# Narrow diagonal tiles behind the products with V, side tasks sorted by the engine that empties their bank, lower parts of queries and keys made behind the next maximum

## The chip, the cores and the metric

The program runs on one core of one Trainium2 chip. The metric is the device time of one execution in microseconds (us). Engines are named as the profile names them: PE is TensorE, DVE is VectorE, ACT is ScalarE, POOL is GpSimd, SP is SyncE, which here only issues transfers.

## The reference

A block of four layers on an input of 2 sequences x 2048 tokens x 256 channels, each with a layer norm ahead of it and a residual sum behind it. The change touches the third, causal attention with 16 heads of 64 channels:

```python
latent_kv = x @ w_kv_down                      # 256 -> 128
k, v = split(latent_kv @ w_kv_up)              # 128 -> 2 x 1024
q = x @ w_q                                    # 256 -> 1024
att = einsum('bqhd,bkhd->bhqk', q, k) * 64 ** -0.5
att = softmax(where(causal, att, -inf))
y = einsum('bhqk,bkhd->bqhd', att, v) @ w_out  # 1024 -> 256
```

Ahead of it stand a state-space layer and a gated token-mixing layer, behind it the token-mixing layer again.

## The kernel before

**Units, tiles and steps.** Attention works on two heads (a pair) and a block of 512 queries at a time: a unit. A sequence has 8 pairs and 4 blocks, so there are 64 units. The unit of block j takes 4(j+1) steps, one for each tile of 128 keys, so a pair has 4 + 8 + 12 + 16 = 40 steps and the whole attention 640. The order of a unit's tiles is the list `TILE[j]`. The last four tiles (numbers 4j to 4j+3) lie on the diagonal: the first of them is as wide as any other (512 queries), the others have 384, 256 and 128. All four need VectorE to lay the causal limit over 128 columns of the scores (`limit`, L1150) before the exponential.

**One step.** The score (L926 to L932): four products for each of the two heads, of the upper and lower parts of keys and queries (`k_hi`, `k_lo`, `q_hi`, `q_lo`) and of the negative maximum, into two PSUM banks. ScalarE takes the exponential into one of four `prob` buffers (L1359), TensorE multiplies it with V into the bank `heads_out` (L947, "weigh"), GpSimd sums it for the denominator (L1438, L1440, L1443, "accumulate").

**Maxima.** Before a unit's scores, its row maxima are taken, some 20 steps ahead: for each tile of 128 queries and block of keys one rough score from the upper parts alone (L903), into banks 5 and 6 (`two_heads`), which VectorE reduces (L1141, and on the diagonal L1138 twice). There are 640 maxima too. They all use this one pair of banks, so a maximum on TensorE waits until VectorE has reduced the maximum before.

**Rounds.** `Plan.attention` writes every engine's order by hand, in rounds of four steps (s = 0, 4, ...). TensorE's order in round s, as a rule:

1. maximum, score s+2, score s+3, maximum (called first and second maximum below)
2. weigh s, s+1, s+2, s+3
3. maximum, score s+4, score s+5, maximum (third and fourth)
4. up to four side tasks ("fillers")

Scores s+4 and s+7 use banks 0 and 1, scores s+5 and s+6 banks 2 and 3. If no side task is open, the fourth maximum is left out and the next round has three maxima. Places are named below by s modulo 40, so a pair has ten rounds, 0, 4, ..., 36; a pair's own steps begin in round 36, whose third part holds its steps 0 and 1.

**Side tasks.** Queries, keys, values, turned maxima, the projection of a unit's result in two halves (`project`), and, once a sequence, latents and turned tiles. In a pair there are 4 queries, 4 keys, 4 turned maxima, 8 halves of projections and on average 4 halves of values. Each has a round from which it is open and one in which it is due. The bank of each is given by its place in the round, `SIDE = [7, 0, 1, 7]`: the first one open goes into bank 7, a second if it is due within 16 steps into bank 0, a third within 8 steps into bank 1, a fourth within 4 into bank 7. A side task in bank 0 or 1 waits for the exponential of step s+4, and score s+7 waits until the side task's bank is emptied. Values and turned maxima are emptied by ScalarE, projections by VectorE (a sum into `X`, L1183). Queries and keys are emptied by both: ScalarE copies the upper part (L1327, L1333), and then VectorE makes the lower part from the bank and the upper part (L1124, L1129).

**Other work on VectorE in the rounds.** `load_out` makes the lower part of the next output weights (L1110), once a pair, ahead of the first maximum; "chores" (`pair_lo`, `values_lo`) make those of other weights behind a maximum; `invert` takes a reciprocal (L1164).

**Ends of a unit.** ScalarE takes the result out of `heads_out` (L1365); 8 steps later GpSimd scales it; 12 steps later `two_parts` splits it, upper part on ScalarE (L1376), lower part on GpSimd (L1452), queued behind the accumulate of step s+1. Projections are open from the next round on.

Of the kernel before, what the change touches and what calls it, by code (L numbers as in the profile page):

```python
# [30 lines left out]
LEAD = 20  # L31
NDEN, QUAD = 8, 32
NG = 3
SIDE = [7, 0, 1, 7]
TILE = [[0, 1, 2, 3], [0, 1, 4, 5, 2, 3, 6, 7], [0, 1, 2, 8, 3, 4, 5, 9, 6, 7, 10, 11], [0, 1, 2, 12, 3, 4, 5, 13, 6, 7, 8, 14, 9, 10, 11, 15]]
DVE_OUT = 62
MIX = [(1, 0), (1, 1), (0, 0), (0, 1)]

# [10 lines left out]
UNITS = [(b, p, j) for b in range(NB) for p in range(NPAIR) for j in range(NBLK)]  # L49
# [30 lines left out]
class Plan:  # L80
# [7 lines left out]
    def __init__(self):  # L88
        self.tasks, self.bank = [], {}
        self.normal, self.stats, self.roots, self.acc = {}, {}, {}, {}  # L90
        self.n_normal = self.n_stats = self.n_roots = self.n_acc = self.step = self.turn = 0
        self.count = [0] * 8
        self.in_steps, self.layers_done, self.done, self.chores = False, False, set(), []
        self.side_bank, self.max_bank = 7, 5
        self.kinds, self.nth, self.masked = {}, {}, {}
        self.start, self.step_of, self.at = [], {}, 0
        self.maxima = [(idx, c, t) for idx, (_, _, j) in enumerate(UNITS) for c in range(j + 1) for t in range(TPB)]
        for idx in range(NU):
            self.start.append(len(self.step_of))
            for t in range(TPB * (UNITS[idx][2] + 1)):  # L100
                self.step_of[idx, t] = len(self.step_of)
        self.freed = [None] * 8
        self.phases()
# [24 lines left out]

    def add(self, *task):
        kind = task[0]  # L130
        self.tasks.append(task)
        self.normal[task] = self.n_normal
        self.kinds[kind] = self.kinds.get(kind, 0) + 1
        self.nth[task] = self.kinds[kind]
        if kind in ("ssm_normal", "turn_normal"):
            self.n_normal += TPB
        elif kind in ("ssm_front", "turn"):
            self.take(task, *([(7,)] * CH if self.in_steps else self.any_bank(CH)))
        elif kind in ("tail_norm", "att_normal"):
            self.n_normal += 2  # L140
        elif kind in ("ssm_states", "ssm_output", "update"):
            self.take(task, *self.any_bank(2))
        elif kind == "products":
            self.take(task, *self.any_bank(4))
        elif kind in ("x_stats", "g_stats"):
            self.stats[task] = self.n_stats
            self.n_stats += 1
        elif kind == "inverse_std":
            self.n_roots += 1
            self.roots[task] = self.n_roots  # L150
        elif kind in ("query", "key", "value", "turn_max", "latent", "denominators", "turn_tiles", "project"):
            self.take(task, self.one_bank())
        elif kind == "maximum":
            self.take(task, (self.max_bank, self.max_bank + 1))
        elif kind == "score":
            n = (0, 2, 2, 0)[self.step_of[task[1:]] % 4]
            if tile_of(*task[1:]) >= TPB * UNITS[task[1]][2]:
                self.masked[task[1:]] = len(self.masked) + 1
            self.take(task, (n, n + 1))
        elif kind == "accumulate":  # L160
            _, idx, t = task
            x0 = left_of(idx, t)
            if t:
                self.n_acc += 2 if t == 1 and x0 else 1
            self.acc[idx, t] = self.n_acc
# [140 lines left out]
    def need(self, *task):  # L306
# [4 lines left out]
        kind = task[0]  # L311
        if kind == "turn_tiles":
            _, b, t = task
# [10 lines left out]
        elif kind == "value":  # L324
            _, vn, half = task
            n, j = divmod(vn, NBLK)
# [15 lines left out]
        elif kind == "maximum":  # L342
            _, idx, c, t = task
            self.need("query", idx)
            self.need("key", idx - UNITS[idx][2] + c)
        elif kind == "fetch_pair" and task[1] >= 2:
            assert all((k, (task[1] - 1) * NBLK - 1) in self.done for k in ("query", "key"))
        elif kind == "fetch_out" and task[1] >= 2:
# [26 lines left out]
            self.chores += [("pair_lo", task[1], i) for i in range(2)]  # L375
        if kind == "load_values":
            self.chores.append(("values_lo", task[1]))

    def chore(self, task):
        self.chores.remove(task)  # L380
# [37 lines left out]
    def attention(self):  # L418
# [22 lines left out]
            if self.chores:  # L441
                self.chore(self.chores[0])

        def filler(latest):
            open_ = sorted((x for x in fillers if x[0] <= s and x[2] not in self.done and early(x[2])), key=lambda x: x[1])
            if open_ and open_[0][1] <= latest:
                fillers.remove(open_[0])
                self.need(*open_[0][2])

        def output(idx):  # L450

# [13 lines left out]
        def early(task):  # L465

            return self.layers_done or task[0] in ("turn_tiles", "latent") or task[1] < {"key": 2, "query": 2, "turn_max": 2, "value": 1}.get(task[0], 0)

        def rows(first, goal, spaced):

            if self.at < goal:
                maximum()
            for n, step in enumerate(steps[first:first + 2]):
                if n and self.at < goal - 1:
                    maximum()
                self.need("score", *step)
            if self.at < goal and spaced:
                maximum()
            else:
                chore()  # L480

        for s in range(-4, len(steps), 4):
# [6 lines left out]
            if s >= 0:  # L489
                goal = min(len(self.maxima), s + 4 + LEAD) if self.layers_done else 0  # L490
                rows(s + 2, goal, True)
                if not s:
                    self.heads_free = self.freed[4]
                for idx, t in steps[s:s + 4]:
                    self.need("weigh", idx, t)
                    self.need("accumulate", idx, t)
                    if (idx, t) == steps[s + 1]:
                        due("two_parts")
                    if t == TPB * (UNITS[idx][2] + 1) - 1:
                        self.need("take_out", idx)  # L500
                        output(idx)
                due("denominators")
                due("scale_out")
                if not s:
                    self.in_steps = False
                    yield
                    self.in_steps = True
            urgent = max([self.start[i] + TPB * (UNITS[i][2] + 1) for i in range(NU) if self.start[i] <= s + 8])
            goal = min(len(self.maxima), max(urgent, s + 6 + LEAD)) if self.layers_done else self.at
            rows(s + 4, goal, any(x[0] <= s and x[2] not in self.done for x in fillers))  # L510
            for n, self.side_bank in enumerate(SIDE):
                filler((10 ** 6, s + 16, s + 8, s + 4)[n])
            self.side_bank = 7
            if self.layers_done and self.at < min(len(self.maxima), s + LEAD):
                maximum()
# [23 lines left out]
def build(nc, u, wA, wF, wKD, wQuery, wValue, wOut, aDiag, h0, gb, mu, out):  # L539
# [4 lines left out]
    with ExitStack() as ctx:  # L544
# [427 lines left out]
        def vector_program(ve):  # L972
# [18 lines left out]
            for task in tasks:  # L991
# [124 lines left out]
                elif kind == "latent":  # L1116
# [1 line left out]
                    cols = slice(j * BLK, (j + 1) * BLK)  # L1118
                    w.wait_ge(lat_hi_ok, b * NBLK + j + 1)
                    ve.tensor_tensor(lat_lo[:, cols], bank(task), lat_hi[:, cols], ALU.subtract).then_inc(empty(task)[0], 1)  # L1120
                elif kind == "query":
                    idx = task[1]
                    w.wait_ge(q_hi_ok, plan.nth[task])
                    ve.scalar_tensor_tensor(out=q_lo[idx % NQ][:, :], in0=bank(task), scalar=DH ** -0.5, in1=q_hi[idx % NQ][:, :],  # L1124
                                            op0=ALU.mult, op1=ALU.subtract).then_inc(empty(task)[0], 1)
                elif kind == "key":
                    idx = task[1]
                    w.wait_ge(k_hi_ok, plan.nth[task])
                    ve.tensor_tensor(k_lo[idx % NKS][:, :], bank(task), k_hi[idx % NKS][:, :], ALU.subtract).then_inc(empty(task)[0], 1)  # L1129
# [431 lines left out]
```

## Time and profile before

| | us |
|---|---|
| median of 3 runs | 2225.58 |
| lowest, highest | 2222.75, 2227.15 |
| profiled execution, its own time | 2222.64 |
| its span in the profile | 2221.3 |
| mean granted TensorE clock (1 is full) | 0.971 |

The span is from the first to the last instruction of the profiled execution; 1.3 us of its time lie around it. Times below count from the start of the span. The attention's rounds run from about 290 us to about 2100 us; a pair takes 109 to 123 us. "Idle before" is the time for which an engine did nothing before an instruction, and the arrow names what ended it.

### The profile page before, as it was taken

To read this page: it belongs to the slowest core of one execution; us is meant where nothing else is said; L and a number is where in the kernel's file an instruction comes from. 1 tells how busy PE (TensorE), PEld (TensorE's weight loads), DVE (VectorE), ACT (ScalarE), POOL (GpSimd) and SP (SyncE) were. 2 spreads that over 40 slices of the span, in tenths; PEclk is the share of its full clock that TensorE was granted. 3 is DMA by queue.
4 is the path that set the end of the run, shared out by engine and by line. 5 is a ranking of instruction groups with operands and counts; after the bars stand their busy time and mean duration, and the time that the engine had idled before them with its cause. 6 is when DMAs were issued, how large, how long until landed. Compare 5 with 4: busy or idle time off the path is not lost.

```text
span 2221.3 us, 33667 instructions
## 1 busy us (share of the span) xinstructions
PE 2004.8 (90%) x12886; PEld 1257.5 (57%) x12886; DVE 1323.7 (60%) x2728; ACT 1077.5 (49%) x1596; POOL 1423.1 (64%) x812
## 2 busy tenths in 40 slices
PE   8987688888999999999988998999899989998889
PEld 6765455545555655555555655555456555554566
DVE  7876655656666555555655556565656565655353
ACT  5775444434444444444454544444444444544575
POOL 1433235776777777777756686766677777777822
PEclk9999799999999999999998999999999999999999
DMA  3000000000000000000000000000000000000001
GB/s 118 1 1 1 0 7 13 17 13 9 18 12 18 9 18 12 18 10 18 12 18 9 11 19 11 17 11 19 11 17 11 19 10 17 11 13 11 25 24 57
DMA packets 29232, 36.90 MB, mean 17 GB/s; under 512 B 6928, under 2 KB 20368, under 8 KB 29072
## 3 DMA queue, kind: packets, MB, share of 16 engines
q1 hardware_dynamic: 29072, 34.76, 5.1%
q8 instruction: 102, 1.67, 0.3%
q14 instruction: 58, 0.48, 0.1%
HBM read 30.02 MB, written 4.46 MB: 16 GB/s over the span
## 4 chain that ended last, share of the span: by engine, by line
PE 54%; DVE 19%; ACT 11%; POOL 9%; issue 6%; DMA 1%; SPq 0%; ACTq 0%; POOLq 0%; DVEq 0%
PE heads_out L947 19%; PE scores L752 7%; PE two_heads L903 7%; POOL acc L1443 6%; PE beside L752 5%; ACT prob L1359 5%; DVE part_max L1141 4%; PE scores L926 3%; PE scores L932 3%; PE scores L930 3%; PE scores L928 3%; DVE two_heads L1138 2%; DVE stats L986 2%; PE two_heads L752 1%; PE beside L958 1%
## 5 line engine op out<-in xcount | busy, mean ns | idle before, releaser
L1443 POOL TENSOR_TENSOR acc<-acc,prob 128x1024 f32<-128x1024 f32 (+3 forms) x512 | 1015.5, 1983 | 236.0 <-ACT prob L1359 189.7
L1359 ACT ACTIVATE prob<-scores 128x1024 f32<-128x1024 f32 (+3 forms) x640 | 550.6, 896 | 632.9 <-PE scores L932 308.8
L1141 DVE TENSOR_REDUCE part_max<-two_heads 128x2 f32<-128x1024 f32 x384 | 468.4, 1220 | 324.7 <-PE two_heads L903 324.1
L947 PE MATMUL heads_out<-prob,V 128*64 128x512 f32 (+3 forms) x2560 | 531.9, 559 | 7.2 <-ACT prob L1359 7.0
L903 PE MATMUL two_heads<-k_hi,q_hi 64*128 64x512 f32 (+3 forms) x1280 | 284.6, 440 | 122.8 <-DVE part_max L1141 78.2
L1138 DVE CUSTOM_DVE_ANT_0 two_heads<-two_heads,mask 128x128 f32<-128x128 f32 (+3 forms) x512 | 241.1, 512 | 250.7 <-PE two_heads L903 250.6
L947 PEld LDWEIGHTS heads_out<-prob,V 128*64 128x64 f32 x2560 | 176.1, 142 | 319.0 <-issue 300.3
L926 PE MATMUL scores<-q_hi,k_hi 64*128 64x512 f32 (+3 forms) x1280 | 246.0, 379 | 30.5 <-ACT prob L1359 17.4
L903 PEld LDWEIGHTS two_heads<-k_hi,q_hi 64*128 64x128 f32 x1280 | 121.2, 185 | 262.6 <-DVE part_max L1141 110.8
L930 PE MATMUL scores<-q_lo,k_hi 64*128 64x512 f32 (+3 forms) x1280 | 236.6, 363 | 0.0
L932 PE MATMUL scores<-neg_max,sel 64*128 64x512 f32 (+3 forms) x1280 | 236.6, 363 | 0.0
L928 PE MATMUL scores<-q_hi,k_lo 64*128 64x512 f32 (+3 forms) x1280 | 236.4, 363 | 0.0
L1438 POOL TENSOR_TENSOR acc<-prob 128x768 f32<-128x768 f32 (+1 forms) x64 | 144.4, 2257 | 126.7 <-ACT prob L1359 103.1
L1452 POOL TENSOR_TENSOR oT_lo<-oT,oT_hi 128x512 fp32r<-128x512 f32 x62 | 78.7, 1269 | 141.8 <-ACT oT_hi L1376 141.8
L926 PEld LDWEIGHTS scores<-q_hi,k_hi 64*128 64x128 f32 x1280 | 123.0, 186 | 77.5 <-issue 26.6
L932 PEld LDWEIGHTS scores<-neg_max,sel 64*128 64x128 f32 x1280 | 123.2, 186 | 18.9
L930 PEld LDWEIGHTS scores<-q_lo,k_hi 64*128 64x128 f32 x1280 | 123.1, 186 | 18.7
L928 PEld LDWEIGHTS scores<-q_hi,k_lo 64*128 64x128 f32 x1280 | 123.1, 186 | 17.0
L1150 DVE TENSOR_TENSOR scores<-scores,limit 128x256 f32<-128x256 f32 x256 | 105.1, 430 | 26.8 <-PE scores L932 26.2
L1365 ACT ACTIVATE oT<-heads_out 128x512 f32<-128x512 f32 x64 | 38.3, 598 | 125.9 <-PE heads_out L947 114.4
L1370 ACT ACTIVATE den_rows<-beside 128x256 f32<-128x256 f32 x64 | 24.6, 384 | 133.7 <-PE beside L958 133.7
L1448 POOL TENSOR_TENSOR oT<-oT,rden 128x512 f32<-128x512 f32 x62 | 79.9, 1289 | 1.9 <-DMA rden<-rden_rows 1.6
(295 smaller groups left out, 2884.1 us busy)
## 6 DMA issues: line engine op xcount, KB each, us to landing
rden<-rden_rows SPq DMA_DIRECT2D x128, 128.0 KB, 2.9
X<-u SPq DMA_DIRECT2D x8, 512.0 KB, 8.9
out<-X SPq DMA_DIRECT2D x8, 512.0 KB, 2.9
wQK_raw<-wQuery SPq DMA_DIRECT2D x16, 192.0 KB, 3.1
wO_raw<-wOut SPq DMA_DIRECT2D x16, 128.0 KB, 2.8
wV_raw<-wValue SPq DMA_DIRECT2D x8, 128.0 KB, 2.7
den<-den_rows SPq DMA_DIRECT2D x64, 4.0 KB
rden_rows<-den SPq DMA_DIRECT2D x64, 4.0 KB, 1.3
```

Of the source, the lines that this page charges most:

```text
L752: made = pe.matmul(dst, l, r, start=first and n == 0, stop=last and n == len(pairs) - 1)
L903: made = pe.matmul(pair_of(task)[:, h, 0:width], q[head(h), t * P:(t + 1) * P], k[head(h), 0:width], start=True, stop=True)
L926: pe.matmul(scores[:, first + h, x0:], k_hi[g][head(h), kc], q_hi[i][head(h), x0:], start=True, stop=False)
L928: pe.matmul(scores[:, first + h, x0:], k_lo[g][head(h), kc], q_hi[i][head(h), x0:], start=False, stop=False)
L930: pe.matmul(scores[:, first + h, x0:], k_hi[g][head(h), kc], q_lo[i][head(h), x0:], start=False, stop=False)
L932: made = pe.matmul(scores[:, first + h, x0:], sel[head(h), :], neg_max[idx % NMAX][head(h), x0:], start=False, stop=True)
L947: made = pe.matmul(heads_out[head(h), x0:], V[vn % NVS][:, tt, p % 2, head(h)], prob[step % NPROB][:, h, x0:], start=t == 0, stop=t == TPB ...
L1138: made = ve.tensor_tensor_reduce(out=pair_of(task)[:, h, 0:width], in0=pair_of(task)[:, h, 0:width], in1=mask[:, BLK - width:], scale=1.0, ...
L1141: made = ve.reduce_max(part_max[:, t, :, c:c + 1], pair_of(task)[:, :, 0:width], AX.X)
L1359: ac.activation(prob[step % NPROB][:, :, x0:], scores[:, first:first + 2, x0:], ACT.Exp).then_inc(empty(task)[0], 1)
L1438: po.tensor_tensor(total[:, :, x0:], old[:, :, x0:], new[:, :, x0:], ALU.add).then_inc(acc_ok, 1)
L1443: po.tensor_tensor(total[:, :, x0:], total[:, :, x0:], new[:, :, x0:], ALU.add).then_inc(acc_ok, 1)
```

## The change

- `TILE`: the narrow diagonal tiles (384, 256 and 128 wide) move to odd places 1, 5, 9, 13 of their unit where they can, so that they are mostly a round's step s+5 in place of its step s+3. Blocks 0 and 1 keep some at even places.
- `SIDE`: each of four places takes only certain kinds. Place one: a projection, into bank 0. Place two: query, key, latent or turned tiles, into bank 7. Place three: value, turned maximum or projection, into bank 1. These take whatever is open, however late it is due. Place four: any kind that is due within 4 steps, into the first of banks 0, 1, 7 that this round has not used.
- A query or key that went into bank 7 no longer has its lower part made by VectorE at its own place in the order; a task `lower` does it behind the first maximum of the next round, or sooner if a task that uses bank 7 or the score's operands asks for it.
- `two_parts` is queued behind the accumulate of step s+2 in place of s+1.

```diff
-SIDE = [7, 0, 1, 7]
-TILE = [[0, 1, 2, 3], [0, 1, 4, 5, 2, 3, 6, 7], [0, 1, 2, 8, 3, 4, 5, 9, 6, 7, 10, 11], [0, 1, 2, 12, 3, 4, 5, 13, 6, 7, 8, 14, 9, 10, 11, 15]]
+SIDE = [([0], ("project",), 99), ([7], ("query", "key", "latent", "turn_tiles"), 99), ([1], ("value", "turn_max", "project"), 99), ([0, 1, 7], None, 4)]
+TILE = [[0, 3, 1, 2], [0, 1, 4, 5, 2, 7, 3, 6], [0, 1, 2, 8, 3, 11, 4, 9, 5, 10, 6, 7], [0, 1, 2, 12, 3, 15, 4, 5, 6, 14, 7, 8, 9, 13, 10, 11]]
...
     def add(self, *task):
         kind = task[0]
+        if self.lowers and self.side_bank == 7 and kind in ("turn_tiles", "latent", "turn_max", "denominators", "query", "key", "value", "project"):
+            self.lower()
...
+            if self.lowers & {("query", idx), ("key", idx - UNITS[idx][2] + c)}:
+                self.lower()
...
+    def lower(self):
+
+        pending, self.lowers = sorted(self.lowers), set()
+        for task in pending:
+            self.add("lower", *task)
+
...
             if self.at < goal:
                 maximum()
+            self.lower()
             for n, step in enumerate(steps[first:first + 2]):
...
-                    if (idx, t) == steps[s + 1]:
+                    if (idx, t) == steps[s + 2]:
                         due("two_parts")
...
-            for n, self.side_bank in enumerate(SIDE):
-                filler((10 ** 6, s + 16, s + 8, s + 4)[n])
+            taken = set()
+            for banks, kinds, ahead_by in SIDE:
+                self.side_bank = next((x for x in banks if x not in taken), 7)
+                if filler(s + ahead_by, kinds):
+                    taken.add(self.side_bank)
+                    if self.side_bank == 7 and self.tasks[-1][0] in ("query", "key") and self.layers_done and s + 4 < len(steps):
+                        self.lowers.add(self.tasks[-1])
+                        self.apart.add(self.tasks[-1])
...
-                elif kind == "query":
+                elif kind == "query" and task not in plan.apart or kind == "lower" and task[1] == "query":
+                    task = task[-2:]
...
-                elif kind == "key":
+                elif kind == "key" and task not in plan.apart or kind == "lower" and task[1] == "key":
+                    task = task[-2:]
```

## Rows read from the trace of the kernel before

**Rows 1.** Busy us from 400 to 2040: PE, PEld, DVE, ACT, POOL; clock.

```profile
400.00:2040.00 1640.00, 1507.16 (x10405) 915.41 (x10405) 976.64 (x1977) 744.88 (x1051) 1193.90 (x652) 0.98 0.05 14
```

**Rows 2.** TensorE's waits from 400 to 2040 us: total, times, longest.

```profile
PE two_heads L903 <- DVE part_max L1141: 68.9, 60, 4.1
PE two_heads L903 <- DVE part_max L1138: 29.0, 57, 1.5
PE scores L926 <- ACT prob L1359: 14.4, 15, 1.0
PE scores L926 <- DVE k_lo L1129: 4.1, 7, 0.7
```

**Rows 3.** Timeline of TensorE and VectorE, an ordinary round: start, length.

```profile
1250.04 0.51 PE L903 MATMUL two_heads<-k_hi,q_hi 64*128 64x512 f32 x2 [0.47 <-DVE part_max L1141]
...
1247.76 0.69 DVE L1129 TENSOR_TENSOR k_lo<-scores,k_hi 128x512 fp32r<-128x512 f32 x1 [0.83 <-ACT k_hi L1333]
1248.37 0.53 DVE L1164 RECIPROCAL den<-den 16x64 f32<-16x64 f32 x1
1248.83 1.15 DVE L1141 TENSOR_REDUCE part_max<-two_heads 128x2 f32<-128x1024 f32 x1
```

**Rows 4.** Timeline of VectorE and TensorE, an output weight's lower part.

```profile
1214.10 1.13 DVE L1110 TENSOR_TENSOR wO_lo<-wO_raw,wO_hi 128x256 fp32r<-128x256 f32 x1
...
1216.42 0.50 PE L903 MATMUL two_heads<-k_hi,q_hi 64*128 64x512 f32 x2 [1.35 <-DVE part_max L1141]
1216.85 4.92 PE L947 MATMUL heads_out<-prob,V 128*64 128x512 f32 x16
```

**Rows 5.** Busy time and granted clock in two stretches of weighs.

```profile
1216.80:1221.80 5.00, 5.00 (x20) 1.56 (x18) 1.23 (x1) 1.11 (x2) 3.60 (x3) 0.66 0.00 0
1203.90:1207.40 3.50, 3.50 (x20) 1.12 (x18) 0.89 (x5) 0.77 (x2) 2.56 (x2) 1.00 0.39 112
```

**Rows 6.** Timeline of TensorE, a round with no side task.

```profile
1333.66 0.39 PE L903 MATMUL two_heads<-k_hi,q_hi 64*128 64x512 f32 x2
1335.03 0.50 PE L926 MATMUL scores<-q_hi,k_hi 64*128 64x512 f32 x2 [0.97 <-ACT prob L1359]
...
1337.78 0.49 PE L903 MATMUL two_heads<-k_hi,q_hi 64*128 64x512 f32 x2 [0.93 <-DVE part_max L1141]
```

**Rows 7.** Timeline of TensorE and ScalarE, scores and first side task.

```profile
1244.68 0.39 PE L903 MATMUL two_heads<-k_hi,q_hi 64*128 64x512 f32 x2
1245.00 0.39 PE L752 MATMUL beside<-wO_hi,oT_hi 128*128 128x256 f32 x1
...
1244.01 1.94 ACT L1359 ACTIVATE prob<-scores 128x1024 f32<-128x1024 f32 x2 [1.00 <-PE scores L932]
```

**Rows 8.** Timeline of TensorE, VectorE and ScalarE where a pair begins.

```profile
1232.38 0.40 PE L932 MATMUL scores<-neg_max,sel 64*128 64x512 f32 x2
...
1233.52 0.50 PE L752 MATMUL beside<-att_xT_hi,wQK_hi 128*128 128x512 f32 x1
...
1232.82 0.43 DVE L1150 TENSOR_TENSOR scores<-scores,limit 128x256 f32<-128x256 f32 x1 [0.37 <-PE scores L932]
...
1233.33 1.73 ACT L1359 ACTIVATE prob<-scores 128x1024 f32<-128x1024 f32 x2 [1.15 <-DVE scores L1150]
```

**Rows 9.** Timeline of TensorE, scores 256 and 128 wide.

```profile
1237.79 0.28 PE L926 MATMUL scores<-q_hi,k_hi 64*128 64x256 f32 x2
...
1238.26 0.23 PE L926 MATMUL scores<-q_hi,k_hi 64*128 64x128 f32 x2
...
1238.55 0.28 PE L932 MATMUL scores<-neg_max,sel 64*128 64x128 f32 x2
```

**Rows 10.** Groups, shapes apart: busy, mean ns, idle before.

```profile
L1359 ACT ACTIVATE prob<-scores 128x1024 f32<-128x1024 f32 x448 | 444.8, 1024 | 461.6 <-PE scores L932 308.8 <-DVE scores L1150 77.4 <-POOL acc L1443 75.1
...
L1452 POOL TENSOR_TENSOR oT_lo<-oT,oT_hi 128x512 fp32r<-128x512 f32 x62 | 78.7, 1269 | 141.8 <-ACT oT_hi L1376 141.8
```

**Rows 11.** VectorE's lower part of an output weight: ns min/median/max.

```profile
L1110 DVE TENSOR_TENSOR wO_lo<-wO_raw,wO_hi x16: 349/1490/1772, 330.4 to 1996.3; 128x256 fp32r<-128x256 f32 x16
```

More of the change, by code:

```diff
@@ L95, in __init__ @@
         self.kinds, self.nth, self.masked = {}, {}, {}
+        self.lowers, self.apart = set(), set()
         self.start, self.step_of, self.at = [], {}, 0
@@ L442, in chore, with filler @@
                 self.chore(self.chores[0])
-        def filler(latest):
-            open_ = sorted((x for x in fillers if x[0] <= s and x[2] not in self.done and early(x[2])), key=lambda x: x[1])
+        def filler(latest, kinds=None):
+            open_ = sorted((x for x in fillers if x[0] <= s and x[2] not in self.done and early(x[2]) and (not kinds or x[2][0] in kinds)), key=lambda x: x[1])
             if open_ and open_[0][1] <= latest:
@@ L448, in filler @@
                 self.need(*open_[0][2])
+                return True
         def output(idx):
```

## The prediction

> **What bounds the kernel.** I read the busy times first, for the stretch of the attention alone. TensorE is busy for 1507 of 1640 us, GpSimd for 1194, VectorE for 977 [rows 1]. So TensorE sets the pace, and what can be won is its idle 133 us and what it loses at a lower clock. Then its waits by what ended them: 97.9 us in 117 waits are maxima waiting for VectorE's reduction of the maximum before, 14.4 us are scores waiting for an exponential, 4.1 us for a key's lower part [rows 2].
>
> Then the timeline, to see which maximum waits. It is the second one of a round, between two scores and the products with V. In [rows 3] VectorE waits 0.83 us for ScalarE's upper part of a key, makes the lower part (0.69), takes a reciprocal (0.53) and only then reduces the first maximum; TensorE stands for 0.47 us. The scores between the two maxima are what hides the reduction, and here the second one is narrow. A score 512 wide takes 0.93 us on TensorE (four products of 0.23), 384 wide 0.71, 256 wide 0.47 (1237.79 to 1238.26), 128 wide 0.40 (1238.26 to 1238.66) [rows 9].
>
> I sort the 97.9 us by kind. The lower part of an output weight once a pair: 1.35 us in [rows 4], where it took 1.13; with its median of 1.49 [rows 11] 1.7, and where ScalarE is late more, so about 28 us over the 14.6 pairs of the stretch. Ordinary waits of 0.3 to 0.5 in six rounds of ten and one of 0.93 every other pair [rows 3, 6]: 3.1 us a pair, 45 us. The other 25 us are long waits behind chores, statistics and latents.
>
> **Tile order and deferred lower parts, for the second maximum.** In the changed order the round's scores s+2 and s+3 are both 512 wide in six rounds of ten, and 768 to 896 in sum in most others, where before eight in ten had a narrow one. In [rows 3], without the key's wait and its 0.69, the reduction starts about when the reciprocal is done, some 1248.1, and ends at 1249.3; TensorE comes at 1249.57. Where the pair of scores was 256 and 128 wide it becomes 512 and 256 or more, 0.53 us or more of added cover. Either is more than the usual 0.3 to 0.5. I take all 45 us as gone; the bounds are 30 and 45. The lower part itself (0.69) goes behind the first reduction, where VectorE otherwise stands until the second maximum; nothing asks for it sooner, as queries and keys are made some 28 steps ahead. Uncovered it would cost 0.69 a time.
>
> The output weight's wait stays: `load_out` still stands ahead of the first maximum. Its scores go from 512 and 256 to 512 and 512, so 0.46 us less: 7 us. The other long waits I leave.
>
> A round without side tasks pays 0.97 at a score and 0.93 at the third maximum behind it [rows 6], every other pair. The new sorting gives this round (32) a turned maximum, which was pulled ahead before; the 0.97 goes: 7 us. Keys no longer sit in banks 0 and 1 as a rule: 4 us. Together 63 us, and with the attention's ends 65.
>
> **Side tasks sorted by bank: what it adds.** Before, the first side task took bank 7 and waited for nothing. Now a projection comes first and takes bank 0, which the exponential of step s+4 must leave. [Rows 7] give its distance with a full score s+5: the exponential starts at 1244.01 and takes 1.02 [rows 10], so it ends at 1245.03, and the side task starts at 1245.00. That is 0.05 late at most. But score s+5 is now mostly narrow, and TensorE arrives earlier by just what the score is shorter. Projections fall into rounds 12, 20, 28 and 36:
> - round 12, 128 wide: 0.93 - 0.40 + 0.05 = 0.6
> - round 20, full: 0.05
> - round 28, 256 wide: 0.93 - 0.47 + 0.05 = 0.5
> - round 36, where a pair begins and the exponential waits for the causal limit: it ends at 1233.33 + 1.02 = 1234.35 [rows 8]. The first side task stood at 1233.52 behind a score 384 wide; behind 128 it stands at 1233.21, so it waits 1.2.
>
> The lone turned maximum of round 32, in bank 1 behind a score 384 wide, waits 0.3. That is 2.65 us a pair, 41 us over 15.5 pairs. Behind it the next round's first maximum comes too soon: two maxima can't start closer than about 1.7 us (0.93 + 0.40 + 0.39 in [rows 6]), and 0.3 of maximum, 0.3 of wait and 0.45 of transposes leave 0.6 to wait: 9.5 us. Cost together 50 us; bounds 20, if the exponentials come earlier, and 60.
>
> TensorE's clock page of the Trainium skill ("TensorE: Matmul & The Clock Gate", on why the gap is 56 ns) has a product of 128 columns start 55.6 ns after the one before at full clock, and four of them would make 0.22 us. The trace disagrees: 0.40 [rows 9], and I go by it. By the page the waits in rounds 12 and 36 would grow by 0.18 each, an estimate of 6 us more and a time of 2214.
>
> **The fourth maximum** also has a narrower score ahead. Where that is 128 wide, the third maximum is mostly one 128 or 256 wide on the diagonal, whose reduction is short. I take 0; the bound is 0.2 us in three rounds of a pair, 9 us.
>
> **`two_parts` behind another accumulate.** GpSimd stood 141.8 us before this task, waiting for ScalarE's upper part [rows 10]; now an addition fills some of that. TensorE waits for GpSimd only through exponentials, little, so I take 0. ScalarE's next take-out may come 0.3 us later: bound 5 us. Shape changes in unit 0's sums move well under 1 us a pair on an engine with slack. No transfer and no wait of the queue on SP is moved past another.
>
> **Clock.** A long wait can be followed by a stretch at the lower level: 16 products took 4.92 us behind the 1.35 us wait [rows 4], at a mean granted clock of 0.66, against 3.5 at 1.00 [rows 5]. A mean of 0.98 [rows 1] means that 4% of the stretch ran at 1.2 GHz and not 2.4, about 32 us lost. Most such waits are long ones, which stay. I take 0; bounds -25, if they vanish, and +22, if the 15 new waits of 1.2 us each bring one at 1.45 us.
>
> **Sum.** 2222.6 - 65 + 50 = 2207.6, against the profiled execution's own time. The median lies 2.9 above that, the profiled one at the low end of the runs, so I say 2209.
>
> **Rivals.**
> - *The side tasks don't wait* (0.20): exponentials come early enough, or the waits replaced others. Then the 65 us stay, 2158, or up to 2180 with half of the waits. For it: the exponential misses a full round by only 0.03 [rows 7]. Against: the arithmetic of widths leaves no room in rounds 12, 28 and 36.
> - *Slower* (0.20): the wait in round 36 is long enough to bring down the clock behind it. The place is the first projection of each pair; the price is 1.45 on top of 1.2. With the fourth maximum's 0.6 the cost per pair becomes 4.7 us, 73 us in all, against 65 won: 2231. It turns at 4.2 us a pair. For it: 1.35 did so in [rows 4]; against: 0.97 and 0.93 in [rows 6] did not.
> - *No change* (0.08): GpSimd, 73% busy, sets the pace of a pair's last unit, and TensorE's won time returns as waits for exponentials: 2223.
> - *The output weight's lower part gets short* (0.05): it takes 0.35 us at the least and 1.49 in the middle [rows 11]. If the shifted sums leave GpSimd idle there, 1.1 a pair goes, 18 us more: 2191. The Trainium skill, "SBUF — State Buffer", on who interferes with whom, names the cause: an operation of VectorE with both inputs in SBUF shares a port with GpSimd's reads, and the loser waits for the other's whole instruction.
> - My forecast (0.47): 2190 to 2220.
>
> **Chances.** Faster by over 0.2% (4.5 us, about what a measurement can tell): 0.47 and 0.05 less 0.05 that lies too near, and 0.20, so 0.67. Same: 0.05 and 0.07 of the 0.08, so 0.12. Slower: 0.20 and the last 0.01, so 0.21. The range takes most of the first rival and the slower one: 2168 to 2236.
>
> **What would show it.** Right: waits of the second maximum near 40 us in place of 98, all long; new waits of side tasks for exponentials, near 40 us, the longest 1.2; q_lo and k_lo without idle time ahead. Wrong: waits for exponentials under 15 us (first rival), or a mean clock under 0.97 (second).

## The result and the profile after

The changed kernel takes 2166.51 us (median of 4 runs, 2162.81 to 2169.17) against 2226.36 for the one before (4 runs): ratio 0.9731, 95% interval 0.9708 to 0.9754. That is 60 us less, just below the range of 2168 to 2236, where 17 us less had been forecast. The profiled execution takes 2169.17 us, 53.5 less than the profiled one before; the mean granted clock rose from 0.971 to 0.978.

First the page, part 1, of the changed kernel, and the view of busy time by stretch (PE, PEld, DVE, ACT, POOL, granted clock). The stretch ends at 1990 us, since TensorE has then had as many instructions as before the change at 2040 (10398 and 10405):

```profile
PE 1978.3 (91%) x12886; PEld 1251.4 (58%) x12886; DVE 1328.0 (61%) x2728; ACT 1074.9 (50%) x1596; POOL 1428.5 (66%) x812
```

```profile
400.00:1990.00 1590.00, 1479.84 (x10398) 908.51 (x10396) 980.77 (x1984) 743.76 (x1051) 1196.56 (x651) 0.99 0.05 14
```

For the same work as in [rows 1] TensorE is idle for 110.2 us and not 132.8, and busy for 1480 and not 1507. Two things became shorter, and the forecast had only the first. On the whole span the busy time fell from 2004.8 to 1978.3, so 26.5 of the 53.5 us are in it. The same instructions ran; they were faster. Part of that is the clock: (1 - clock) times the span, the time lost at 1.2 GHz as an estimate, falls from 64 us (0.971 of 2221.3) to 48 us (0.978 of 2167.9). The other 10 us are taken up below, behind no_side.

TensorE's waits in that stretch (total, times, longest):

```profile
PE two_heads L922 <- DVE part_max L1162: 37.0, 37, 2.7
PE scores L771 <- ACT prob L1380: 33.9, 57, 1.1
PE two_heads L922 <- DVE part_max L1159: 8.7, 24, 1.3
PE beside L771 <- DVE q_lo L1144: 5.2, 7, 1.0
PE scores L945 <- ACT prob L1380: 3.5, 6, 0.6
PE two_heads L922 <- DVE q_lo L1144: 3.0, 2, 1.5
PE beside L868 <- DVE k_lo L1150: 2.8, 2, 1.4
```

Against [rows 2]: maxima wait 45.7 us and not 97.9, scores 3.5 and not 18.5. New are 33.9 us of side tasks waiting for exponentials, and 11 us in which something waits for the lower part of a query or key. The timeline of TensorE shows the new waits in one pair (start, length, in brackets the idle time and what ended it):

```profile
1299.43 0.38 PE L771 MATMUL scores<-wO_hi,oT_hi 128*128 128x256 f32 x1 [0.29 <-ACT prob L1380]
1304.18 0.49 PE L922 MATMUL two_heads<-k_hi,q_hi 64*128 64x512 f32 x2 [0.77 <-DVE part_max L1162]
1310.38 0.66 PE L930 MATMUL scores<-ident,row_max 128*128 128x128 f32 x4 [0.27 <-ACT prob L1380]
1311.54 0.49 PE L922 MATMUL two_heads<-k_hi,q_hi 64*128 64x512 f32 x2 [0.50 <-DVE part_max L1162]
1320.37 0.38 PE L771 MATMUL scores<-wO_hi,oT_hi 128*128 128x256 f32 x1 [1.07 <-ACT prob L1380]
```

They are rounds 28 (a projection), 32 (the second maximum, then the lone turned maximum and the maximum behind it) and 36 (a projection). Round 12 of an earlier pair:

```profile
1127.69 0.39 PE L771 MATMUL scores<-wO_hi,oT_hi 128*128 128x256 f32 x1 [0.64 <-ACT prob L1380]
```

The forecast had 0.5 for round 28, 0.3 and 0.6 for the turned maximum of round 32 and the maximum behind it, 1.2 for round 36 and 0.6 for round 12; the trace has 0.29, 0.27, 0.50, 1.07 and 0.64. The second maximum of round 32, the one behind the output weight's lower part, is where the forecast was far off: 0.77 and not some 1.5.

### The profile page after: what moved, and what is told of

It is laid out like the page before. It is cut to its first block, busy times and chain, and to the rows that moved or that the text cites. A ratio compares the mean times of both kernels' runs of the same rounds, so it can differ in the third digit from the quotient of the medians.

```text
span 2167.9 us, 33697 instructions
## 1 busy us (share of the span) xinstructions
PE 1978.3 (91%) x12886; PEld 1251.4 (58%) x12886; DVE 1328.0 (61%) x2728; ACT 1074.9 (50%) x1596; POOL 1428.5 (66%) x812
## 4 chain that ended last, share of the span: by engine, by line
PE 70%; DVE 16%; ACT 9%; issue 3%; POOL 1%; DMA 1%; SPq 0%; ACTq 0%; DVEq 0%; POOLq 0%
PE heads_out L966 22%; PE scores L771 11%; PE two_heads L922 8%; PE beside L771 6%; PE scores L945 4%; PE scores L951 4%; PE scores L949 4%; PE scores L947 4%; ACT prob L1380 4%; DVE part_max L1162 3%; DVE two_heads L1159 2%; PE two_heads L771 2%; PE beside L977 2%; DVE stats L1005 2%; DVE X L1204 1%
## 5 line engine op out<-in xcount | busy, mean ns | idle before, releaser
L1464 POOL TENSOR_TENSOR acc<-acc,prob 128x1024 f32<-128x1024 f32 (+3 forms) x512 | 1034.8, 2021 | 368.7 <-ACT prob L1380 330.9
L966 PE MATMUL heads_out<-prob,V 128*64 128x512 f32 (+3 forms) x2560 | 517.3, 546 | 3.8 <-ACT prob L1380 3.7
L966 PEld LDWEIGHTS heads_out<-prob,V 128*64 128x64 f32 x2560 | 167.9, 139 | 278.4 <-issue 241.4
L945 PE MATMUL scores<-q_hi,k_hi 64*128 64x512 f32 (+3 forms) x1280 | 239.9, 370 | 9.1 <-ACT prob L1380 6.7
L1459 POOL TENSOR_TENSOR acc<-prob 128x256 f32<-128x256 f32 (+1 forms) x64 | 126.7, 1980 | 78.5 <-ACT prob L1380 77.7
L1171 DVE TENSOR_TENSOR scores<-scores,limit 128x256 f32<-128x256 f32 x256 | 106.2, 428 | 63.0 <-PE scores L951 61.2
L1204 DVE TENSOR_TENSOR X<-X,scores 128x512 f32<-128x512 f32 x127 | 87.0, 686 | 82.0 <-PE scores L771 80.8
L771 PE MATMUL scores<-wO_hi,oT_hi 128*128 128x256 f32 x254 | 79.0, 311 | 31.9 <-ACT prob L1380 31.4
```

The source lines that it names most:

```text
L771: made = pe.matmul(dst, l, r, start=first and n == 0, stop=last and n == len(pairs) - 1)
L945: pe.matmul(scores[:, first + h, x0:], k_hi[g][head(h), kc], q_hi[i][head(h), x0:], start=True, stop=False)
L966: made = pe.matmul(heads_out[head(h), x0:], V[vn % NVS][:, tt, p % 2, head(h)], prob[step % NPROB][:, h, x0:], start=t == 0, stop=t == TPB ...
L1459: po.tensor_tensor(total[:, :, x0:], old[:, :, x0:], new[:, :, x0:], ALU.add).then_inc(acc_ok, 1)
L1464: po.tensor_tensor(total[:, :, x0:], total[:, :, x0:], new[:, :, x0:], ALU.add).then_inc(acc_ok, 1)
```

## The experiments

All were timed in 3 rounds beside the kernel before on the same chip. "Maxima" is the sum of TensorE's waits for VectorE's reductions over the whole span in the run's view of waits, "exp." that of the group of L752 (projections and other products; L766 to L773 in the variants) waiting for an exponential, "out lo" the median length of VectorE's operation for the output weight's lower part (`wO_lo`).

| run | us | ratio, 95% interval | clock | maxima us | exp. us | out lo ns |
|---|---|---|---|---|---|---|
| before | 2226.36 | 1 | 0.971 | 122.0 | 0.3 | 1490 |
| after | 2166.51 | 0.9731, 0.9708 to 0.9754 | 0.978 | 68.1 | 36.6 | 1216 |
| tile_only | 2167.61 | 0.9765, 0.973 to 0.98 | 0.982 | 90.2 | 0.6 | 1566 |
| side_only | 2251.6 | 1.0139, 1.0104 to 1.0175 | 0.967 | 123.0 | 15.4 | 2378 |
| lower_only | 2238.33 | 1.0074, 1.0051 to 1.0097 | 0.965 | 121.5 | 0.3 | 2212 |
| two_only | 2223.54 | 1.0009, 0.9988 to 1.0029 | 0.966 | 115.7 | 0.3 | 426 |
| no_tile | 2203.99 | 0.9899, 0.9881 to 0.9918 | 0.967 | 96.6 | 15.6 | 1631 |
| no_side | 2163.32 | 0.9717, 0.9699 to 0.9736 | 0.977 | 73.4 | 0.6 | 590 |
| no_lower | 2191.58 | 0.9846, 0.9831 to 0.9861 | 0.979 | 75.9 | 36.0 | 719 |
| no_two | 2161.94 | 0.9744, 0.9709 to 0.978 | 0.978 | 59.2 | 36.1 | 526 |
| after_stall | 2198.92 | 0.988, 0.9861 to 0.9899 | 0.972 | 89.4 | 36.6 | 1444 |
| before_out_chore | 2191.37 | 0.9863, 0.9831 to 0.9895 | 0.971 | 95.7 | 0.3 | 862 |
| before_out_pool | 2187.08 | 0.9856, 0.9826 to 0.9886 | 0.973 | 95.1 | 0.3 | on GpSimd |
| after_out_chore | 2148.7 | 0.9668, 0.9637 to 0.9699 | 0.984 | 55.1 | 36.1 | 946 |
| after_swap | 2136.68 | 0.9617, 0.9578 to 0.9657 | 0.977 | 68.6 | 11.0 | 1218 |
| after_swap_out | 2121.96 | 0.9548, 0.9509 to 0.9586 | 0.979 | 57.4 | 10.5 | 950 |
| after_swap_pool | 2110.77 | 0.9512, 0.9483 to 0.9542 | 0.982 | 50.1 | 12.6 | on GpSimd |
| no_side_pool | 2145.82 | 0.967, 0.9643 to 0.9698 | 0.98 | 61.2 | 2.7 | on GpSimd |

The runs were timed in sets, and the kernel before had medians of 2220.84 to 2226.36 in them, so runs of different sets are compared by their ratios. The clock and the last three columns are those of the profiled execution.

### One part of the change alone

**tile_only**: the `TILE` line of the change, everything else as before.

> The kernel before with the new tile order alone. First theory (waits of the second maximum are covered by the wider scores ahead of it, and nothing is paid at side tasks because the first of them still takes bank 7): the second maximum's 98 us of waits fall to about 50, no side task waits for an exponential, and with about half of the low-clock stretches gone the time is 2170 to 2182. Rival (the tile order only moves the wait to the fourth maximum, and the gain comes from the deferred lower parts): 2212 to 2226.

2167.61 us: the tile order alone gives what the whole change gives. Maxima wait 32 us less, side tasks wait 0.6 us in all for an exponential, and the clock is 0.982. The first theory holds in its main point; the time lies 2 us below its range. Its sizes were off: between 400 and 1990 us the maxima still wait 67.9 us (52.0 and 15.9) and not about 50, and the clock gives more. The stretches at 1.2 GHz between 400 us and the end of that work are 16 before, 6 here and 6 after the change.

**side_only**: the `SIDE` line and its loop, without `self.lowers.add` and `self.apart.add`.

> The kernel before with the new sorting of side tasks alone: old tile order, lower parts at once. First theory (a projection in bank 0 waits for the exponential of step s+4 only where score s+5 is narrow or the exponential is late by the causal limit): waits of side tasks of about 15 us, nearly all in the round where a pair begins, against 10 to 15 us won at rounds without side tasks: 2212 to 2226. Rival (sorting by the emptying engine is what frees VectorE): 2180 to 2200.

2251.6 us, slower than either theory. The side tasks' 15 us are as expected. What was missing stands in the last column: the output weight's lower part takes 2.38 us and not 1.49. The second maximum behind it waits about 2.4 us and not about 2, though other maxima win that back (123.0 us in all against 122.0). The rest of the loss is busy time, 2018.2 us against 2004.8, in part at the lower clock (0.967).

**lower_only**: the deferral in the old loop.

```diff
             for n, self.side_bank in enumerate(SIDE):
-                filler((10 ** 6, s + 16, s + 8, s + 4)[n])
+                if filler((10 ** 6, s + 16, s + 8, s + 4)[n]):
+                    if self.side_bank == 7 and self.tasks[-1][0] in ("query", "key") and self.layers_done and s + 4 < len(steps):
+                        self.lowers.add(self.tasks[-1])
+                        self.apart.add(self.tasks[-1])
```

> The kernel before with deferred lower parts alone, for queries and keys that the old sorting puts into bank 7. First theory (only some queries and keys are in bank 7 there, and the narrow scores ahead of the second maximum remain): waits of the second maximum fall by 10 to 20 us, time 2200 to 2215. Rival (VectorE's wait for ScalarE's upper part is the cause of most waits): they fall by 40 us or more, 2165 to 2185.

2238.33 us, 0.7% slower; both theories fall. The maxima wait as long as before, and again the output weight's operation grew, to 2.21 us. The timeline of VectorE and of GpSimd in this run shows what its length hangs on:

```profile
1090.86 2.52 DVE L1126 TENSOR_TENSOR wO_lo<-wO_raw,wO_hi 128x256 fp32r<-128x256 f32 x1 [0.58 <-ACT wO_hi L1316]
...
1090.72 2.38 POOL L1461 TENSOR_TENSOR acc<-acc,prob 128x1024 f32<-128x1024 f32 x1
```

VectorE's operation begins 0.14 us after an addition of GpSimd and ends 0.28 us after it (1093.38 and 1093.10). In the kernel before, same place of the program:

```profile
1082.72 1.72 DVE L1110 TENSOR_TENSOR wO_lo<-wO_raw,wO_hi 128x256 fp32r<-128x256 f32 x1 [0.59 <-ACT wO_hi L1298]
...
1081.77 2.38 POOL L1443 TENSOR_TENSOR acc<-acc,prob 128x1024 f32<-128x1024 f32 x1
```

It begins later in the addition and ends again 0.29 us after it (1084.44, 1084.15). In the changed kernel:

```profile
1059.15 1.19 DVE L1129 TENSOR_TENSOR wO_lo<-wO_raw,wO_hi 128x256 fp32r<-128x256 f32 x1
...
1057.67 2.39 POOL L1464 TENSOR_TENSOR acc<-acc,prob 128x1024 f32<-128x1024 f32 x1
```

Later still, and the same 0.28 us behind. This operation has both inputs in SBUF. Alone it takes 0.35 us at the least [rows 11]; beside an addition it lasts until 0.28 us behind the addition's end, so its length is what is left of that addition. Each edit that shifts one engine against the other changes it, and with it the wait of the second maximum. So the one-part runs below and above never change one thing alone: the last column of the table has to be read with each.

**two_only**: `steps[s + 1]` becomes `steps[s + 2]` for `two_parts`.

> The kernel before with two_parts behind the accumulate of step s+2 alone. First theory: GpSimd's idle time before this task falls from 142 us to under 20, and TensorE doesn't notice: 2220 to 2229. Rival (GpSimd's delay reaches VectorE through ScalarE's late upper parts, and so the maxima): 2195 to 2212.

2223.54 us, no difference that can be measured, and GpSimd's idle time before this task falls to 7.4 us, as the first theory has it. But TensorE does notice; the effects cancel. The output weight's operation:

```profile
L1124 DVE TENSOR_TENSOR wO_lo<-wO_raw,wO_hi x16: 350/426/2503, 330.1 to 1999.4; 128x256 fp32r<-128x256 f32 x16
```

The median of 0.43 us hides two kinds of pair: from the fourth on it takes 0.42 to 0.43 us in seven and 2.45 to 2.50 us in five. The second maximum behind it waits 0.8 us in six of the seven and 2.8 us in the five. TensorE's idle time is 8 us less than before, its busy time 7 us more, at a clock of 0.966.

### The change without one part

**no_tile, no_side, no_lower, no_two**: the changed kernel with the old `TILE` line; with the old sorting, the deferral kept as in lower_only; without the two lines that add to `self.lowers` and `self.apart`; with `steps[s + 1]`.

> The changed kernel with the old tile order. First theory (the tile order brings most of the gain and most of the side tasks' waits): waits of side tasks for exponentials fall from 35 us to about 15, waits of the second maximum rise to 65 to 80, time 2190 to 2210. Rival (the other parts carry the gain): 2162 to 2175.

2203.99 us: the other three parts give 1.0% together, the tile order the rest. The first theory holds: exponentials 15.6 us, maxima 74.3 us (59.2 and 15.1) between 400 and 2025 us.

> The changed kernel with the old sorting of side tasks. First theory (the new sorting costs some 35 us of waits for exponentials and wins some 15 to 20): side tasks wait under 3 us, time 2145 to 2165. Rival (the sorting is needed for the gain, since it puts all queries and keys into bank 7): 2172 to 2195.

2163.32 us, the same as the change within the intervals, though the side tasks' 36 us are gone. So the sorting wins about as much as it costs. I had it winning 11 us. TensorE's busy time has the difference: in this run it is idle 22.5 us less than after the change and busy 17.4 us more (1995.7 against 1978.3), at nearly the same clock. Part of the 22.5 is the output weight's operation, 0.59 us here against 1.22. In tile_only, also with the old sorting, busy times by stretch are:

```profile
400.00:1990.00 1590.00, 1492.45 (x10367) 901.68 (x10365) 982.50 (x1971) 746.39 (x1048) 1197.11 (x649) 0.99 0.05 14
```

12.6 us more than after the change, for 31 instructions fewer, at the same clock. One source can be seen. With the old sorting a score is held up by a query's lower part in its bank so shortly that no idle time is recorded. TensorE before the change, with the round 8 in which `q_lo` in bank 0 ends at 1269.54:

```profile
1269.14 0.39 PE L932 MATMUL scores<-neg_max,sel 64*128 64x512 f32 x2
1269.60 0.50 PE L926 MATMUL scores<-q_hi,k_hi 64*128 64x512 f32 x2
1269.93 0.39 PE L928 MATMUL scores<-q_hi,k_lo 64*128 64x512 f32 x2
```

Start to start is 0.46 us where a product takes 0.23: 0.23 us lost, hidden behind the modelled end of the product before.

Busy time less the clock's part, estimated for each profiled execution as in the section on the result, sorts the runs: 1940 us before, 1953 in tile_only, 1946 in no_side, 1945 in no_lower, but 1931 after the change and 1929 in no_tile. New sorting and deferral together take some 10 us of such hold-ups out of the kernel before and some 20 out of tile_only. That all of it is this one kind of hold-up is not shown.

> The changed kernel with lower parts made at once. First theory (the wider scores already cover the reduction in most rounds, so deferring adds little): 2168 to 2180. Rival (deferring is what removes the waits): 2190 to 2210.

2191.58 us, in the rival's range: in company with the new sorting and the new tile order the deferral is worth 1.2%. The profiled executions are 18.6 us apart; 12.4 us of that are busy time and 6.2 idle, so most of it is hidden hold-ups and not, as the rival has it, waits. The maxima wait only 8 us longer here, but that is with an output weight's operation of 0.72 us and not 1.22; at the places behind it they wait 7 us less, elsewhere 15 us more. With the old sorting and old tile order the deferral brought no gain (lower_only, where that operation grew).

> The changed kernel with two_parts back behind the accumulate of step s+1. First theory (moving it shifts the phase of GpSimd's additions, and by that the length of VectorE's output-weight operation): that operation's length changes from 1.24 us to another value between 0.4 and 2.5 us and the second maximum's wait in round 32 changes by the same amount; time 2150 to 2190, in proportion to it. Rival (GpSimd's order is without effect on VectorE): 1.24 us stays and the time is 2163 to 2170.

2161.94 us, and `wO_lo` takes 0.53 us and not 1.22, the maxima's waits fall by 9 us. The phase of GpSimd's additions shifted and shortened VectorE's operation, as the first theory has it. A gain in time can't be told: by ratio the run is no faster than the change (0.9744 against 0.9731, intervals overlapping).

### The wait behind the output weight

**before_out_chore** and **after_out_chore**: VectorE makes this lower part behind a maximum.

```diff
         if kind == "load_values":
             self.chores.append(("values_lo", task[1]))
+        if kind == "load_out":
+            self.chores.append(("out_lo", task[1]))
...
-                elif kind == "load_out":
+                elif kind == "out_lo":
```

(the second edit in the program of VectorE alone)

> The kernel before with one edit: VectorE makes the output weight's lower part behind a maximum, as it does with the other weights, and no longer ahead of the first maximum of the round. First theory (this one wait, once a pair, costs its 2 us and the low clock behind it): idle time falls by 20 to 28 us and the time in low-clock stretches by another 12 to 20, time 2180 to 2195. Rival (idle time alone): 2198 to 2206.

2191.37 us: one wait a pair, 26 us of idle time in all, was worth 31. The idle time and the time are as in the first theory. Its clock part isn't there in its size: the profiled executions have the same clock (0.971), and busy times of 2002.1 and 2004.8 us.

> The changed kernel with the same edit. Its wait there is 0.8 us and no low-clock stretch follows it. First theory: only the idle time goes, 12 us, 2152 to 2158. Rival (it brings clock too): under 2148.

2148.7 us, 0.6% less than the change; the waits fall by 13 us. It lies between the theories: the idle time of the first, and a little clock besides (0.984 in the profiled execution, the fastest of four; 0.980 to 0.982 in the others).

**before_out_pool**: the same operation on GpSimd, at its old place in the order.

```diff
-                    ve.tensor_tensor(wO_lo[n % 2][:, :], wO_raw[n % 2][:, :], wO_hi[n % 2][:, :], ALU.subtract).then_inc(wO_ok, 1)
+                    po.tensor_tensor(wO_lo[n % 2][:, :], wO_raw[n % 2][:, :], wO_hi[n % 2][:, :], ALU.subtract).then_inc(wO_ok, 1)
```

> The kernel before with one edit: GpSimd in place of VectorE makes the output weight's lower part, at the same place of the task order. First theory (this operation on VectorE lasts until the addition that GpSimd is in has ended, and that is what the second maximum waits for): on GpSimd it takes under 0.8 us each time, the second maximum's wait in round 32 falls from 2.1 us to 0.3 or less, idle time falls by 25 to 30 us and the time is 2182 to 2194. Rival (the wait comes from ScalarE's late upper part and from the projections' sums): the wait in round 32 stays above 0.8 us and the time above 2205.

2187.08 us. This operation's view (ns min/median/max):

```profile
L1443 POOL TENSOR_TENSOR wO_lo<-wO_raw,wO_hi x16: 722/738/743, 328.2 to 1965.4; 128x256 fp32r<-128x256 f32 x16
```

On GpSimd it always takes 0.72 to 0.74 us, and TensorE's idle time falls by 26 us, as the first theory has it. But the run doesn't part the two theories: with the operation VectorE also loses its standing for ScalarE's upper part, the 0.59 us in the row at 1082.72. That was 8.2 us in 12 times before the change. The other part, VectorE held by GpSimd, is what its operation takes beyond 0.42 us, some 14 us over the 16 pairs.

**after_stall**: the reverse, idle time put back.

```diff
                 elif kind == "load_out":
                     n = task[1]
                     w.wait_ge(wO_hi_ok, n + 1)
+                    w.wait_ge(att_const, 4)
+                    for i in range(2):
+                        ve.reduce_max(spare[:, i:i + 1], mask[:, :], AX.X)
```

> The changed kernel with two reductions of a constant into an unused column added on VectorE once a pair, just ahead of the output weight's lower part, about 1.25 us. They lengthen the wait of the second maximum there from 0.8 us to about 2.0, what it was before the change; nothing else is changed. First theory (the waits above about 1.3 us are what brings TensorE to the lower clock): 15 x 1.25 = 19 us more idle time and 10 to 22 us more in low-clock stretches, which go from 7 to 15 or more between 400 and 2040 us; 2197 to 2207. Rival (the clock came back because all idle time together shrank): idle time alone, 2183 to 2190, and the clock stays at 0.98.

2198.92 us: the maxima wait 21.3 us more, the time is 32 us longer, and the clock falls from 0.978 to 0.972. The time and its division are the first theory's: a third of the price of such a wait is the clock behind it. The stretches at 1.2 GHz between 400 and 2040 us are 10 and not the 15 or more that it had.

### The order of side tasks

**after_swap**: a query or key first, then the projection.

```diff
-SIDE = [([0], ("project",), 99), ([7], ("query", "key", "latent", "turn_tiles"), 99), ...
+SIDE = [([7], ("query", "key", "latent", "turn_tiles"), 99), ([0], ("project",), 99), ...
```

> The changed kernel with the first two places of side tasks exchanged: the query or key in bank 7 first, then the projection in bank 0. First theory (the projection's wait for the exponential is a matter of order: a query is 1.4 us and a key 0.7 us of work): the waits of 0.64 us in round 12 and 1.07 us in round 36 go, 24 us of idle time, and the time is 2140 to 2152. Rival (the projection's sum then comes late on VectorE and the second maximum waits in its place): 2160 to 2170.

2136.68 us, by ratio 1.2% below the change and 3 us below the first theory's range. The waits for exponentials fall from 36.6 to 11.0 us and nothing takes their place (maxima 68.6 against 68.1). The working of these waits, exponential against the width of the score, was right, and they can be had back by order alone.

**after_swap_out**: after_swap and after_out_chore together.

> Both edits, the exchange and the output weight's lower part behind a maximum. First theory: they add up, 36 us of idle time, 2128 to 2142. Rival (what one wins the other has won already): 2145 to 2155.

2121.96 us, 6 us below the first theory's range: they add up (1.9% by ratio, against 1.2% and 0.6%).

**after_swap_pool** and **no_side_pool**: `load_out`, `pair_lo` and `values_lo` of VectorE's program moved into GpSimd's, with `po` for `ve`.

> The changed kernel with the first two places of side tasks exchanged and the lower parts of all weights (output, values, queries and keys) made by GpSimd. First theory: the waits of the second maximum behind the output weight (0.8 us a pair) and behind the value weight (2.15 us in six rounds) go; GpSimd has the time; 2110 to 2122. Rival (GpSimd comes late with a pair's query and key weights, or its longer sums hold exponentials): 2125 to 2150.

2110.77 us, 4.9% below the kernel before, the fastest of this study. First theory.

> The new tile order, deferred lower parts and place of two_parts with the old sorting of side tasks, and all weights' lower parts on GpSimd. First theory (the old sorting has no waits for exponentials at side tasks at all, but its rounds without side tasks cost 1.7 us each and values 0.7): 2125 to 2142. Rival (sorting by the emptying engine pays once the projection isn't first): slower than the run with the exchange by 10 us or more.

2145.82 us, 1.7% more than after_swap_pool. So the rival holds: sorting by the emptying engine pays, once the projection isn't first and the weights' lower parts are on GpSimd.

## Why the prediction was wrong

**What bounds the kernel.** Right: TensorE's waits behind narrow scores, and the clock.

**The miss.** Against the profiled execution before, the forecast had 15 us less and 53.5 were measured. Of the 38 us between, some 17 are clock, some 10 busy time that isn't clock, and 12 idle time (26.9 us less on the whole span, 216.5 to 189.6, against 15).

**Tile order.** Right. Waits of maxima went from 97.9 to 45.7 us, 52 us less. The sum had 42.5: 45 and 7 won, 9.5 lost behind the lone turned maximum. Most of the rest is the output weight's wait, below. Scores wait 15 us less; the sum had 11. tile_only shows that this part alone brings as much as the whole, with the clock.

**Side tasks.** Right in place and nearly in size: 33.9 us against 41, and 0.50 behind the lone turned maximum against 0.6. Missed were the 11 us in which a task in bank 7 or a maximum asks for a lower part, about half of it a fourth side task of round 36. Deferring is not what makes most of them: no_lower, which defers nothing, has 9.6 us of these waits.

**Clock: the step that failed.** "Most such waits are long ones, which stay. I take 0." TensorE's busy time fell by 26.5 us, and some 17 of them are clock (64 us lost before, 48 after). The other 10 us are hold-ups that leave no idle time, for which the sum had no term and which the view of waits couldn't show. What was wrong is that a long wait was priced without its clock in either direction: before_out_chore and before_out_pool win 1.2 us for each us of it that they remove, after_stall pays 1.5. The long waits did not all stay, either: behind the output weight's lower part eleven of 1.8 to 2.1 us became 0.74 to 0.80.

That this shortening brought the 17 us is not shown, and the traces speak against it as the main cause. Only two of the eleven were followed by the lower level within 4 us in the profile before. The runs that remove the wait won 2.7 and 6.8 us of busy time. And in tile_only these waits are still 1.4 to 1.8 us, while the clock's loss is the least of the three (39 us); with the old tile order, in no_tile, it is 73 us. The wait in [rows 4] itself is 1.29 us after the change where it was 1.35, now without a low stretch behind it. So the clock came back with the tile order, and through which waits stays open.

**Output weight.** The second step that failed. I took 0.46 us off its wait, for the width, 7 us in all, and gave 0.05 to the case that its operation gets short. Between 400 us and the end of the attention the waits at this place fell by 15 us (31.4 to 16.2). The operation did get shorter, 1.19 to 1.25 us in these eleven pairs where it took 1.47 to 1.77, because it now begins later in GpSimd's addition. VectorE also no longer stands there for ScalarE's upper part (0.6 us in all, 8.2 before).

**Rivals.** The time fell among those of the first rival (2158 to 2180), but its reason fell: side tasks wait 33.9 us, and under 15 was its sign. The slower rival had round 36's wait bring down the clock. The wait is there (1.07 us), the clock is higher. Its 4.7 us a pair also left out one of two terms of 0.6; with both it is 5.3. The wait in round 12 is 0.64, which fits 0.40 us for a score 128 wide (0.6). It doesn't fit the 0.22 (0.8) that the prediction estimated from the Trainium skill ("TensorE: Matmul & The Clock Gate", on why the gap is 56 ns).

**What each part did** could not be read from the sum of parts. Alone, sorting costs 1.4% and deferring 0.7%, but in both runs the output weight's operation grew by 0.7 to 0.9 us. With the new tile order sorting is neutral. Deferring pays with the new sorting: 1.2% with the new tile order, and with the old one no_tile is 2.4% below side_only, though `two_parts` moves and that operation gets 0.75 us shorter there too.

## What to carry to other kernels

When a wait on the bounding engine is priced, price what follows it too: here 21 us of added waits of about 2 us cost another half of their length in clock, and removing 26 us of them gave back another fifth. An operation of VectorE with both inputs in SBUF beside a busy GpSimd has no length of its own; move it to GpSimd, or to where nothing waits, before tuning around it, and check its length in every run that is to show something else. And when side tasks borrow a bank, put first the one whose bank is already free.

## What the hardware showed unexpectedly

- VectorE's subtraction of two SBUF tensors took from 0.35 to 2.52 us. In the 15 traces where VectorE makes it there are 240; 168 began inside an operation of GpSimd and ended 0.28 to 0.29 us after that one's end. 61 began while GpSimd ran nothing and took 0.35 to 0.43 us. The other 11 took 0.41 to 0.43 us and began in the first 4 ns or the last 50 ns of one. This is the Trainium skill's rule ("SBUF — State Buffer", on who interferes with whom): the loser waits for the other's whole instruction. The traces agree but for those at the edges, and add the 0.28 us. The lower parts of queries and keys, with one input in PSUM, took 0.67 to 0.70 us throughout.
- How often a wait of TensorE was followed by the lower level, counted over 14 of the traces (before, after and all variants but no_two and the three with GpSimd making lower parts) between 400 and 2000 us, as a stretch at 1.2 GHz that began during the wait or within 4 us of its end: 5 of some 710 waits of 0.3 to 0.6 us, 11 of 61 of 1.3 to 1.5 us, 36 of 120 of 1.5 to 1.9 us, 23 of 35 of 1.9 to 2.1 us, 27 of 48 of 2.1 to 2.4 us, 36 of 48 above 2.4 us. Length alone doesn't decide it.
- A hold-up of TensorE of 0.23 us can leave no idle time in the profile, since it hides in the modelled end of the product before.
